# Attention in a fused transformer kernel: queries and keys split at the border of image and text

## The reference

```
Q = _rope(x @ Wq.T + bq)
K = _rope(x @ Wk.T + bk)
V = x @ Wv.T + bv
A = einsum('btd,bsd->bts', Q, K) / sqrt(256)
A = where(causal, A, -inf);  A = softmax(A, axis=-1)
out = einsum('bts,bsd->btd', A, V) @ Wf.T + bf
...
logits = xf @ wr + br
topk_vals, topk_idx = top_k(logits, 2);  gates = softmax(topk_vals)
```

## Time and profile before

| | us |
|---|---|
| three runs, median | 890.33 (890.0 to 891.31) |
| the profiled execution | 891.11, of which the span of the records is 889.3 |
| PE busy | 776.2 (87% of the span) |
| DVE busy | 521.9 (59%) |
| ACT and POOL busy | 366.0 and 366.2 (41% each) |
| mean granted clock of PE | 0.935 of full |

### The profile page before, as it was taken

One profiled execution on the slowest core, in us unless ns is written; L12 is line 12 of the kernel. 1 busy time (PEld: TensorE's weight loads), 2 busy tenths in 40 slices (PEclk: granted clock), 3 DMA queues, 4 the chain that ended last, 5 costly groups with the idle time before them and its releaser, 6 DMA issues.

```text
span 889.3 us, 17678 instructions
## 1 busy us (share of the span) xinstructions
PE 776.2 (87%) x5506; PEld 609.1 (68%) x5507; DVE 521.9 (59%) x1300; ACT 366.0 (41%) x795; POOL 366.2 (41%) x314
## 2 busy tenths in 40 slices
PE   3898904999999999478999998958999999999991
PEld 2677802666666666356777776747898999999981
DVE  5898888433333333286777877884555555555550
ACT  5795671333333333224343343503444444444430
POOL 3349931223232322134455552012555555555442
PEclk9998965999999999878999997977999999999996
DMA  9950132232121111331111211521233332232325
GB/s 259 417 200 1 66 123 91 68 76 30 30 30 30 30 30 25 95 118 46 50 47 51 67 47 47 182 76 38 43 51 51 48 48 48 48 48 48 42 25 145
DMA packets 37042, 66.98 MB, mean 75 GB/s; under 512 B 3552, under 2 KB 29264, under 8 KB 35312
## 3 DMA queue, kind: packets, MB, share of 16 engines
q1 hardware_dynamic: 22992, 47.16, 15.9%
q0 software_dynamic: 13824, 19.01, 13.7%
q10 hardware_dynamic: 192, 0.38, 0.1%
HBM read 45.49 MB, written 23.74 MB: 78 GB/s over the span
## 4 chain that ended last, share of the span: by engine, by line
PE 75%; DVE 12%; POOL 5%; ACT 2%; DMA 2%; issue 1%; SPq 0%; POOLq 0%; DVEq 0%; ACTq 0%
PE PS L899 14%; PE PS L707 14%; PE PS L912 14%; PE PS L725 7%; PE PS L1208 5%; POOL X L1794 4%; PE PS L1218 3%; PE PS L1227 2%; PE PS L715 2%; PE PS L1256 2%; PE PS L1246 1%; PE PS L885 1%; DMA Y<-in_wtok_dram 1%; PE PS L1248 1%; PE PS L1969 1%
## 5 line engine op out<-in xcount | busy, mean ns | idle before, releaser
L1051 POOL DMA_INDIRECT sum<-X,dest x48 | 97.4, 2029 | 107.4 <-ACT X L966 95.3
L707 PE MATMUL PS<-X,Y 128*128 x576 | 134.3, 384 | 1.3 <-DVE Y L805 1.3
L912 PE MATMUL PS<-X 128*128 x768 | 133.5, 273 | 1.8 <-ACT X L966 1.8
L899 PE MATMUL PS<-X 128*128 128x256 f16 x768 | 130.2, 275 | 1.5 <-DVE X L984 1.5
L956 ACT ACTIVATE X<-PS,X 128x256 f32<-128x256 f32 x192 | 75.3, 475 | 109.9 <-PE PS L899 109.9
L899 PE MATMUL PS<-X,Y 128*128 128x256 f16 x384 | 105.5, 275 | 0.0
L912 PE MATMUL PS<-Y,X 128*128 x384 | 104.7, 273 | 0.0
L816 DVE SCALAR_TENSOR_TENSOR Y<-PS,Y 128x512 f32<-128x512 f32 x48 | 36.1, 751 | 111.5 <-PE PS L707 111.5
L871 POOL DMA_INDIRECT sum<-Y,dest x24 | 38.1, 1586 | 148.0 <-ACT Y L782 148.0
L707 PEld LDWEIGHTS PS<-X,Y 128*128 128x128 f16 x576 | 56.9, 99 | 60.8 <-issue 4.3
L899 PEld LDWEIGHTS PS<-X 128*128 x768 | 75.6, 99 | 11.4 <-issue 2.1
(11 more groups left out here) (356 smaller groups left out, 1499.1 us busy)
## 6 DMA issues: line engine op xcount, KB each, us to landing
X<-in_w_dram SPq DMA_DIRECT2D x11, 1024.0 KB, 17.4
stage<-in_w_dram SPq DMA_DIRECT2D x16, 512.0 KB, 3.5
sum<-h SPq DMA_DIRECT2D x2, 2048.0 KB, 7.5
xs<-Y SPq DMA_DIRECT2D x2, 1040.0 KB, 5.0
xs<-Y SPq DMA_DIRECT2D x2, 1032.0 KB, 5.5
h<-in_txt_dram SPq DMA_DIRECT2D x2, 1024.0 KB, 18.3
Y<-in_patches_dram SPq DMA_DIRECT2D x3, 672.0 KB, 8.8
sum<-h SPq DMA_DIRECT2D x2, 768.0 KB, 3.9
```

What stands on the lines that cost most here:

```text
L707: ins = nc.tensor.matmul(PS[:, 2 * u + s, 0:F0], x_[:, slot, k, :], w_[:, at_:at_ + F0], start=(n == 0), stop=(n == 3 * KC - 1))
L899: ins = nc.tensor.matmul(PS[:, 2 * s + c // 2, (c % 2) * T1:(c % 2 + 1) * T1], part[:, off:off + P], x_[:, slot, k, :], start=(n == 0), st ...
L912: ins = nc.tensor.matmul(PS[:, 4 + a, 0:D], h_[:, s, c, a * P:(a + 1) * P], part[:, off:off + D], start=(s == 0 and c == 0 and n == 0), st ...
L1051: nc.gpsimd.indirect_dma_start(out=sum1, out_offset=bass.IndirectOffsetOnAxis(ap=dest[:, i:i + 1], axis=0), in_=y1buf[:, i // 2 % 2, i % 2 ...
```

## The change

Five things change together.

1. **Split at the border.** Group A is now the 128 text tokens against all 165 keys, group B the 37 image tokens against the 37 image keys. Scores, maxima, exponentials, transposes and values follow that. The values of the text and the router's four columns are one product of 260 columns (`wvx`, in bank 2); the image's values are written beside queries and keys in banks 0 and 1 (`SIDE`), 128 columns each. Because of these banks, `project(b+1)` waits at its start for `v_copied` of the sequence before.
2. **Text divided at the sum.** The text's probabilities aren't divided by their sum; `add_text` multiplies the output by the reciprocal. The factor for the maxima (`nmax`) moves from DVE to ACT, which then waits for itself (`max_negated`).
3. **Residual regrouped.** First tiles 0 and 16 are loaded, then 1, 2, 3 and 17, then the rest. The moments are taken for these three groups, the last (16 tiles) in `batch(2)`, with `maxima(2)` inside the wait for the root. Image tiles 18 to 21 are normalised in `batch(2)` to `batch(5)` and transposed beside text tiles 4 to 7. `project(0)` stands before the transposes of tiles 17 and 1. Six sequences are unrolled (`START`).
4. **Running sums.** `first_max` is a reduce, a compare, a scan and one more operation (4 for 9); the three adds and the memset in `positions` are one scan.
5. The attention's weights are loaded by six DMAs in place of three (with their semaphore's count raised from 48 to 96), and POOL adds the image bias in sequences 6 to 11.

```diff
-BACK = (((BATCH, 1), (0, 4)), ((BATCH + 1, IT - 1),), ((4, BATCH - 4),))
+BACK = (((0, 2, BATCH),), ((1, 3, 1), (BATCH + 1, 1, 1)), ((4, BATCH - 4, 1), (BATCH + 2, IT - 2, 1)))
+START = 6
...
         def first_max(chain, values, top, hot, equal, count):
...
             chain.link(nc.vector.tensor_reduce(top, values.rearrange("p g t -> p t g"), AX, ALU.max))
-            chain.link(nc.vector.tensor_tensor(hot, values, over(top, 4), ALU.is_equal))
-            taken = newt
-            chain.link(nc.vector.tensor_copy(taken, hot[:, 0, :]))
-            for g in range(1, 4):
-                chain.link(nc.vector.tensor_tensor(hot[:, g, :], hot[:, g, :], taken, ALU.is_gt))
-                chain.link(nc.vector.tensor_tensor(taken, taken, hot[:, g, :], ALU.max))
+            chain.link(nc.vector.tensor_tensor(tokens(equal), values.rearrange("p g t -> p t g"),
+                                               top.unsqueeze(2).broadcast_to([P, NT, 4]), ALU.is_equal))
+            chain.link(nc.vector.tensor_tensor_scan(by_token(count), restart.rearrange("p t g -> p (t g)"), by_token(equal), 0.0,
+                                                    ALU.mult, ALU.add))
+            chain.link(nc.vector.scalar_tensor_tensor(out=hot.rearrange("p g t -> p t g"), in0=tokens(count), scalar=1.0,
+                                                      in1=tokens(equal), op0=ALU.is_equal, op1=ALU.mult))
...
             def project(b, slot):
...
+                wait_from(pe, v_copied, b)
                 for bank, w_, done in ((0, wq, q_psum), (1, wk, k_psum)):
+                    for k in range(KC):
+                        nc.tensor.matmul(PS[0:IMG, bank, SIDE:SIDE + P], xTb[:, slot, k, 0:IMG],
+                                         wvx[:, k, bank * P:(bank + 1) * P], start=(k == 0), stop=(k == KC - 1))
...
-                    if bank == 0:
-                        for k in range(KC):
-                            ins = nc.tensor.matmul(PS[:, 0, BASE_AT:BASE_AT + E1], xTb[:, slot, k, IMG:SEQ], wr1[:, k, :],
...
-                wait_from(pe, v_copied, b)
-                for a, (c0, c1) in enumerate(((0, P), (P, SEQ))):
-                    for k in range(KC):
-                        ins = nc.tensor.matmul(PS[0:c1 - c0, 2, a * D:(a + 1) * D], xTb[:, slot, k, c0:c1], wv[:, k, :],
+                for k in range(KC):
+                    ins = nc.tensor.matmul(PS[:, 2, 0:PAY1], xTb[:, slot, k, IMG:SEQ], wvx[:, k, :],
...
             def scores(b, slot):
...
-                for o_, q0, q1, k1 in ((0, 0, P, P), (P, P, SEQ, SEQ)):
+                for o_, q0, q1, k1 in ((0, IMG, SEQ, SEQ), (SEQ, 0, IMG, IMG)):
...
             def exps(b):
                 act.wait_ge(s_max, b + 1)
+                nc.scalar.activation(nmax, smax, ACT.Copy, scale=-SCALE).then_inc(max_negated, 1)
+                act.wait_ge(max_negated, b + 1)
...
             def maxima(b):
                 dve.wait_ge(s_psum, b + 1)
-                nc.vector.tensor_tensor(sA1, PS[:, 3, 0:P], k_maskA, ALU.add)
...
-                chain.link(nc.vector.tensor_reduce(smax[:, 0:1], sA1, AX, ALU.max))
-                nc.vector.tensor_scalar(nmax, smax, -SCALE, None, ALU.mult).then_inc(s_max, 1)
+                nc.vector.tensor_tensor(sB1[0:IMG, :], PS[0:IMG, 3, SEQ:SEQ + IMG], k_causal[0:IMG, 0:IMG], ALU.add)
+                chain.link(nc.vector.tensor_tensor_reduce(sA1, PS[:, 3, 0:SEQ], k_mask, 1.0, -3e38, ALU.add, ALU.max, smax[:, 0:1]))
+                nc.vector.tensor_reduce(smax[0:IMG, 1:2], sB1[0:IMG, :], AX, ALU.max).then_inc(s_max, 1)
...
-                nc.vector.tensor_scalar(pA, pA, rsum[:, 0:1], None, ALU.mult)
...
+                nc.vector.scalar_tensor_tensor(out=hb, in0=PS[:, 6, 0:D].unsqueeze(1), scalar=whole, in1=hb,
+                                               op0=ALU.mult, op1=ALU.add).then_inc(h3_added, 1)
...
-            stats_of((BATCH, 0, 1, 2, 3))
-            moments_back(0, BATCH + 1, (BATCH, 0, 1, 2, 3), 5)
+            stats_of((0, BATCH))
+            moments_back(0, BATCH + 1, (0, BATCH), 2)
             norm_image(0)
             norm(0, 0, 0)
+            dve.wait_ge(h_loaded[1], 16 * len(BACK[1]))
+            stats_of((1, 2, 3, BATCH + 1))
+            moments_back(1, BATCH + 1, (1, 2, 3, BATCH + 1), 6)
+            norm_image(1)
             norm(1, 1, 1)
...
-            moments_back(BATCH + 1, IT - 1, range(BATCH + 1, NT), IT + 4)
-            for n in range(1, IT):
-                norm_image(n)
...
             def batch(b, slot):
-                maxima(b)
+                if known(b, 2):
+                    moments_back(4, NT - 4, rest_, NT, lambda: maxima(2))
+                else:
+                    maxima(b)
```

More of the change, by code:

```diff
@@ L593, in positions @@
             chain.link(nc.vector.tensor_reduce(tl, full, AX, ALU.add))
-            chain.link(nc.vector.memset(st[:, 0:1], 0.0))
-            for g in range(1, 4):
-                chain.link(nc.vector.tensor_tensor(st[:, g:g + 1], st[:, g - 1:g], tl[:, g - 1:g], ALU.add))
+            chain.link(nc.vector.tensor_tensor_scan(st[:, 1:4], onesf[:, 0:3], tl[:, 0:3], 0.0, ALU.mult, ALU.add))
             chain.link(nc.vector.tensor_scalar(sl, st, float(P * unit), None, ALU.mult))
@@ L1077, in sp_rest @@
             for k, parts in enumerate(BACK):
-                for t, n in parts:
-                    sp.dma_start(h[:, t:t + n, :], sum0[t * P:(t + n) * P].rearrange("(t p) n -> p t n", p=P))\
+                for t, n, step in parts:
+                    tiles = slice(t, t + (n - 1) * step + 1, step)
+                    sp.dma_start(h[:, tiles, :], sum0[0:TOKENS].rearrange("(t p) n -> p t n", p=P)[:, tiles, :])\
                         .then_inc(h_loaded[k], 16)
@@ L1170, in heads @@
         def heads(eng, body):
-            body(0, 0)
-            body(1, 1)
-            with eng.Fori(1, BATCH // 2 - 1) as j:
+            for b in range(START):
+                body(b, b % 2)
+            with eng.Fori(START // 2, BATCH // 2 - 1) as j:
                 body(2 * j, 0)
@@ L1191, in image, with beside @@
                 ins.then_inc(xi_tr, 1)
+            def beside(n):
+                pe.wait_ge(xi_ready, n + 1)
+                for k in range(KC):
+                    ins = nc.tensor.transpose(PS[:, 7, BESIDE + k * P:BESIDE + (k + 1) * P], xnF[:, 2 + n, k * P:(k + 1) * P],
+                                              k_ident)
+                return ins
             def text(b, slot):
@@ L1198, in text @@
                     ins = nc.tensor.transpose(PS[:, 7, k * P:(k + 1) * P], xnF[:, slot, k * P:(k + 1) * P], k_ident)
+                if isinstance(b, int) and 4 <= b < IT + 2:
+                    ins = beside(b - 2)
                 ins.then_inc(xn_tr, 1)
@@ L1280, in base_images @@
             def base_images():
+                pe.wait_ge(v_copied, BATCH)
                 for n in range(IT):
@@ L1366, in act_attention @@
             text(0, 0)
+            roots(1, BATCH + 1)
+            image(1)
             text(1, 1)
-            roots(BATCH + 1, IT - 1)
-            for n in range(1, IT):
-                image(n)
             def run(b, slot, j):
+                if known(b, 2):
+                    roots(4, NT - 4)
                 exps(b)
                 copy_pt(b)
-                if known(b, 1):
-                    roots(4, BATCH - 4)
                 if not (isinstance(b, int) and b >= BATCH - 2):
@@ L1381, in run @@
                 chunk(b, slot, j)
-            run(0, 0, 0)
-            run(1, 1, 0)
-            with act.Fori(1, BATCH // 2 - 1) as j:
+            for b in range(START):
+                run(b, b % 2, b // 2)
+            with act.Fori(START // 2, BATCH // 2 - 1) as j:
                 run(2 * j, 0, j)
@@ L1424, in pool_attention @@
             bias(1)
-            for n in range(IT):
-                image_bias(n)
             for b in range(BATCH):
@@ L1563, in logit_base @@
                 chain.link(nc.vector.tensor_tensor(raw1, raw1, old, ALU.add))
-            batch(0, 0)
-            batch(1, 1)
-            with dve.Fori(1, BATCH // 2 - 1) as j:
-                chain.begin(j - 1, 6)
+            for b in range(START):
+                batch(b, b % 2)
+            with dve.Fori(START // 2, BATCH // 2 - 1) as j:
+                chain.begin(j - START // 2, 4)
                 batch(2 * j, 0)
                 batch(2 * j + 1, 1)
-                chain.end(BATCH // 2 - 2)
+                chain.end(BATCH // 2 - 1 - START // 2)
             batch(BATCH - 2, 0)
             batch(BATCH - 1, 1)
-            add_text(BATCH - 1)
+            add_text(BATCH - 1, 1)
             dve.wait_ge(stats_ready, NT + BATCH)
```

152 lines of the change are left out of this document (83 added, 69 removed).

## The result

The changed kernel takes **866.97 us** (median of four runs, 864.91 to 870.52) against 890.33 before: a ratio of 0.9737, with a 95% interval of 0.9704 to 0.9770. A fourth run of the kernel before took 4457.89 us and is left out. Five more runs of the changed kernel gave 868.01 against 890.03 in nine runs of the kernel before (0.9752, 0.9735 to 0.9769). The prediction was 868.1, range 861 to 875. The profiled execution took 870.52 us (span 868.7) against 891.11 (span 889.3): 20.6 us less, where the sum said 22.2.

The account below looks back on a forecast made before the run. TensorE's own stream was taken to bound steady sequences, with waits at the start, end and second routing. Terms summed to 22.2 us off the profiled 891.11, giving 868.9; the median, 0.8 lower, was forecast at 868.1, range 861 to 875.

Parts of the forecast that it names:

- Before the attention, -0.4: First mixture's routing: only the adds replaced by a scan count, since VectorE waits for ScalarE's sigmoid anyway; 0.4 us saved.
- Projection 0 and scores 1, -10.0: Attention's start: smaller first load, fewer statistics and moments, image tiles deferred; scores 1 at 393.4, 10.0 us earlier.
- Scores 0 at 385 instead of 388.4: Attention's start: after projection 0 at 378.1 and queries ready at 380.9, the first scores start at 385.
- Sequence 1, -4.3: Interval from scores 1 to scores 2: twelve moments, the root and its table load go; 8.8 us, 4.3 saved.
- Sequence 2, -1.5: Next interval: moments of 16 tiles and two ScalarE table loads lose 0.9; 10.1 us against 11.6, 1.5 saved.
- The loop, -3.2: Sequences 3 to 15: period 8.96 for 9.28 us; less two more image transposes in three bodies, 3.2 us saved.
- The steps' price: TensorE's cost of switching weight width: 0.12 us from wide to 37-wide weights, 0.2 us back.
- The last sequence, -1.5: Attention's end: L1485, 1.48 us in GpSimd's shadow, leaves the chain; transposes 3.95 us after the scores, not 5.45.
- Routing 2, -1.3: Second mixture's routing: 0.85 us from the best-expert search, limited by ScalarE's table load, and 0.45 from the adds; 1.3 saved.
- The clock didn't stay up at the end: Rival about the attention's end: less idle time keeps TensorE at full clock, 5.0 us more saved, 863 us; chance 0.18.
- the start gives less: Rival: the first load lands at 375.9 and the clock drops once more in a gap; 872 us; chance 0.15.
- the ring of VectorE and GpSimd: Rival: rotary products, GpSimd's sum, scores, maxima and next normalised tile bound the loop at 10.7 us; 894 us; chance 0.03.

Follow-up runs that it names:

- d_start: Changed kernel plus 41 useless products on TensorE in its waits at the start of the attention; 865.14 us.
- seq2: Changed kernel with ScalarE's sequence 1 weight chunk and the root's table load moved behind copies of transposed probabilities, GpSimd's subtraction behind the rotary sums; 865.75 us.
- together: Changed kernel with the image's values in one narrow group before the queries and the value product's narrow halves before its wide ones; 857.77 us.
- probs_undone: Changed kernel with the text's probabilities divided before the transposes again and the factor for the maxima back on VectorE; 866.37 us.

## Why the prediction was right

The time was right to 1.1 us, but that is in part luck: terms were off both ways and cancelled, and the runs of one kernel lie 3 to 5.6 us apart. In the profiled pair the sum of 22.2 came out as 20.6 us: up to scores 1 8.0 in place of 10.4, sequences 1 and 2 6.3 for 5.8, the loop 5.1 for 3.2, and behind scores 15 1.2 for 2.8.

- **Before the attention, -0.4.** Measured -0.7 at the first expert tile, of which 0.51 are the running sums; the rest is less than the scatter. By the first load's issue only 0.3 of it is left, and that is contained in the -8.0 below.
- **Projection 0 and scores 1, -10.0.** Measured 403.40 to 395.43, **-8.0**. The load, the statistics and projection 0 came as worked out. The step that failed is "Scores 0 at 385 instead of 388.4". From the queries' end (forecast 380.9, measured 381.5) to scores 0 it let 4.1 us; the image's values and the keys alone took 3.2 of it (1.00 and 2.19), where at full clock they take 1.9, and the rotary products and the sum another 2.3. So it let the keys run at full clock, and the clock rose only at 384.2. `d_start` gave the missing 2 us back, and 1 us more.
- **Sequence 1, -4.3.** 13.2 to 8.8 us, right. **Sequence 2, -1.5.** 11.6 to 9.7, -1.9: the queue of ScalarE stood as told, and its cost was 0.66 and not 0.9 over a sequence with image transposes (seq2).
- **The loop, -3.2.** Measured 111.1 to 105.9 us from scores 3 to 15, **-5.1**. The mis-sized term is the transposes of the probabilities: +0.11 a sequence was forecast, -0.11 came (0.48 before, 0.11 + 0.11 + 0.15 now). Before, they stood behind a product with 37-wide weights (the values of the last 37 text tokens), and the first took 0.26 (row below); now they stand behind the wide text product, and it takes 0.11. The prediction counted 11 steps before and after; this one, of 0.15, it had priced nowhere. The other terms were right to 0.03 each, 0.05 too low together, so that 0.17 a sequence is left, twelve times: scores 0.83 for 0.80, image's values 0.44 and 0.56 for 0.43 and 0.55, text's values 0.88, value product 1.78 for 1.79, the two transposes beside the text 0.22. The transposes in the kernel before, same chain view:

```profile
526.98 0.26 PE PS L1235
527.25 0.18 PE PS L1236
527.43 0.04 PE PS L1237
```

- **The steps' price** of 0.12 in and 0.2 back holds in the projection (0.32 for a pair in `together`); in the value product it is 0.2 each way, as the prediction's 1.79 had it (0.39).
- **The last sequence, -1.5.** Measured 5.44 to 3.78, -1.7, but the reason was partly wrong: the prediction credited that L1485 leaves the chain, and probs_undone puts such an operation back (0.17 us) at a loss of 0.2. What counts there is that the maxima end before GpSimd starts. In sequences 1 and 2, which the prediction did not name for it, the same operation took 1.66 and 1.62 us, and part 2 gave 0.5 us.
- **Routing 2, -1.3.** Measured 1.35, with ScalarE as the bound, as told. But from scores 15 to the second experts only 2.0 of these 3.0 us arrive: the half clock begins 4.3 us behind the scores and not 5.1, and takes in 5.1 us of the first expert tile where it took in 3.8. This was in no term. Behind the start of the second experts the changed kernel loses another 0.8 us.
- **Rivals.** The clock didn't stay up at the end, and its price of 5.0 looks too high by what was seen (3.0 at most, with 3.4 us of half clock left). Of "the start gives less", the load landed early and the clock did not fall again; the part that came true is that it stayed down. The period was 8.79, not 9.28, and the ring of VectorE and GpSimd was no bound even at 8.08.

## What to carry to other kernels

When TensorE bounds a loop, count the changes between wide and narrow weights over the whole round, including the group that the next one follows, and put narrow groups next to each other: four changes were worth 0.71 us here. Before crediting an earlier start, look at the granted clock there: 1.8 us of an earlier load became about 1, and useless products in the wait gave 3.0. When runs of one kernel differ by 3 us, compare places in the trace and not only medians, and compare with several kernels that are unedited there: here one reference row made a gain of 1.1 to 4.2 us look like 4.2.

## What the runs showed of the hardware

- Where GpSimd's 128x1024 subtraction runs, even a 37x37 division on VectorE takes 0.88 us (0.25 without it) and ends with the subtraction. A normalised image tile takes 0.81 us beside GpSimd's 128x256 additions and 0.41 alone.
- TensorE was given full clock from the expert tiles to the end of the loop when it was kept at work in the pause of the first load, and fell to half behind 24 products of four columns, even with about 1 us of wide products right behind them.
- A narrow group costs its follower too: the first 128-wide transpose takes 0.26 us behind a 37-wide group and 0.11 behind a full one.
